# A cross-attention kernel on one core: a second PSUM bank for the second head's context, softmax weights read back in one transfer, and both value products ahead of the contexts

## The chip, the core and the metric

The kernel runs on one core of one Trainium2 chip. The number that counts is the device time in microseconds (us) of one execution. A core has TensorE (PE, matrix products into PSUM), VectorE (DVE), ScalarE (ACT), GpSimd (POOL) and SyncE (SP), whose queue issues the DMA transfers here. Each engine works through its own list of instructions in order, and the lists are tied by semaphores that the program waits for. PSUM has eight banks of 512 fp32 values per partition, named here by number.

## The reference, cut to what matters

Sixteen sequences of 128 tokens and 512 features pass one RWKV layer (its time mix and channel mix come first in the kernel and are not touched) and then a block with two cross-attentions and an MLP. The context `xf` is 128 tokens per sequence:

```
def _cross_attention(q_in, kv_in, wq, bq, wk, bk, wv, bv, wo, bo, bias_k, bias_v):
    qh = (q_in @ wq + bq).reshape(b, q_len, H, K)          # H = 16 heads of K = 128
    kh = (kv_in @ wk + bk).reshape(b, t, H, K)
    vh = (kv_in @ wv + bv).reshape(b, t, H, K)
    kh = concatenate([kh, bias_k], axis=1)                 # a 129th key and value
    vh = concatenate([vh, bias_v], axis=1)
    weights = softmax(einsum('bqhk,bthk->bhqt', qh, kh) / sqrt(K))
    ctx = einsum('bhqt,bthk->bqhk', weights, vh)
    return ctx @ wo + bo
...
x = x + attention_1(layer_norm(x), xf); x = x + attention_2(layer_norm(x), xf)
x = x + gelu(layer_norm(x) @ w_fc1 + b_fc1) @ w_fc2 + b_fc2
```

## The kernel before, in words

`cross_attend` works in units. A unit is two heads of four sequences (a "quad", 512 tokens). Sixteen sequences make two halves `h`; a half has two quads; each attention `st` has 8 pairs of heads `g`. That makes 2 x 2 x 8 x 2 = 64 attention units. Products that must be exact are made of three passes with split operands (`_hi` and `_lo`, helper `mm3`, lines 60 to 62).

Each engine has its own function for one step of the pipeline, and the step joins two units: `A`, whose attention is finished, and `C`, whose queries, keys and values are made meanwhile. `slot(A, C)` is the step inside a half's attention: 7 turns of a loop, 2 steps each, four times, 56 in all. The other 8 are at borders, where a layer norm for the next stage goes between: `second` (4 times, the second quad of a stage), `turn` (2, from attention 1 to 2) and `mlp_turn` (2, to the MLP; the last of them has no unit `C`). On PE `second` and `turn` are both `passing`.

The order within a step is written out by hand on each engine. On PE in `slot`: the scores of A's two heads among queries and keys of C, then `value(C, 0)` (bank 2), `context(A, 0)`, half of `value(C, 1)` (bank 3), `context(A, 1)`, the other half, and `attended(A)`, the output product. One `value` call is 24 matmuls of 256 columns.

Softmax weights take a detour. ScalarE writes `exp` into `pr` with queries on partitions; VectorE normalises (line 1741) and transposes blocks of 32 x 32 (line 1745) into `pb`; SyncE's queue stores `pb` to DRAM (line 1441) and loads it back with whole keys on partitions into `pT` (line 1446, a tile that the profile calls `xres`). `context` (line 1991, `ca_ps<-xres,xq`) multiplies it with the values `vT` (`xq`) into `BANK_PV`, bank 7, for both heads. ScalarE reads that bank into `ct_hi` (line 1559), VectorE reads it again for `ct_lo` (line 1749), and `context` waits, by `ct_split`, until the head before it has been read. `attended` waits for `ct_lo` of head 0 before its first matmul and of head 1 before its fourth (line 60, `ca_ps<-ca_wo_hi,ca_ct_hi`).

Of the kernel before, what the change touches and what calls it, by code (L numbers as in the profile page):

```python
# [20 lines left out]
ACT = mybir.ActivationFunctionType  # L21
# [4 lines left out]
P = 128  # L26
# [1261 lines left out]
def cross_attend(nc, io, x3, out, common, early):  # L1288
    HT = 8
    G = NH // 2  # L1290
    KW = L + 1
    BANK_Q, BANK_K, BANK_O, BANK_SC, BANK_PV = 0, 1, 2, 5, 7
    TB = 32
    LN_BANKS = (0, 1, 5, 6)
    FC_BANKS = ((4, 7), (5, 6))
# [1 line left out]
    with ExitStack() as ctx:  # L1297
# [119 lines left out]
        def head_col(U, kind, hd):  # L1417
            return hv[:, bass.ds(U.g * 2 + ((U.st * 5 + HV[kind]) * NH + hd), 1)]
# [4 lines left out]
        def _(sp):  # L1423
# [13 lines left out]
            def probs_across(A, hd):  # L1437

                sp.wait_ge(blocks_ready, A.n * 2 + (hd + 1))
                sp.wait_ge(pt_in[hd], A.n * 64)  # L1440
                sp.dma_start(pb_dram[hd], pb[hd][:].rearrange("p j b s -> p (j b s)")).then_inc(blocks_out[hd], 16)
                if A.n > 0:
                    sp.wait_ge(pv_full, A.n * 2 + (hd - 1))
                sp.wait_ge(blocks_out[hd], A.n * 16 + 16)
                for j in range(4):
                    sp.dma_start(pT[hd][TB * j:TB * j + TB, :].rearrange("r (i x) -> r i x", i=4),  # L1446
                                 pb_dram[hd].rearrange("(i r) (j x) -> j r i x", i=4, j=4)[j]).then_inc(pt_in[hd], 16)

            def probs(h, i, quad):
                for hd in range(2):  # L1450
# [77 lines left out]
        def _(act):  # L1528
# [27 lines left out]
            def context_hi(A, hd):  # L1556
                act.wait_ge(pv_full, A.n * 2 + (hd + 1))
                wait_apart(act)
                act.activation(cT[hd][0][:], ps[:, BANK_PV, :], ACT.Identity, bias=head_col(A, "bias_v", hd)).then_inc(ct_hi, 1)  # L1559

            def roots(ln):
                act.wait_ge(stats_ready, ln + 1)
                act.activation(std[:, :], mv[:, :, 1], ACT.Sqrt, bias=eps[:]).then_inc(std_ready, 1)
# [35 lines left out]
            def second(A, C):  # L1599
                exps(A, 0)  # L1600
                key_out(C, 0)
                split_one(wo, so, wo_in, wo_hi, C.wq)
                exps(A, 1)
                key_out(C, 1)
                roots(C.ln)
                context_hi(A, 0)
                split_one(wk, sk, wk_in, wk_hi, C.wkv + 1)
                context_hi(A, 1)
                norm_hi(C.ln, C.st, 1)
                query_out(C, 0, BANK_Q)  # L1610
# [96 lines left out]
        def _(v):  # L1707
# [29 lines left out]
            def normalise(A, hd):  # L1737
                v.wait_ge(exp_done, A.n * 2 + (hd + 1))
                v.reciprocal(rss[hd][:], sms[hd][:]).then_inc(rs_done, 1)
                v.wait_ge(rs_done, A.n * 2 + (hd + 1))  # L1740
                v.tensor_tensor(pr[hd][:, :, 0:L], pr[hd][:, :, 0:L],  # L1741
                                rss[hd][:].rearrange("p (a b) -> p a b", b=1).broadcast_to([P, 4, L]), ALU.mult).then_inc(norm_done, 1)
                v.wait_ge(norm_done, A.n * 2 + (hd + 1))
                v.wait_ge(blocks_out[hd], A.n * 16)
                v.transpose(pb[hd][:].rearrange("p j b s -> p b j s"), pr[hd][:, :, 0:L].rearrange("p b (j s) -> p b j s", s=TB)).then_inc(blocks_ready, 1)  # L1745

            def context_lo(A, hd):
                v.wait_ge(ct_hi, A.n * 2 + (hd + 1))
                v.scalar_tensor_tensor(out=cT[hd][1][:], in0=ps[:, BANK_PV, :], scalar=head_col(A, "bias_v", hd),  # L1749
                                       in1=cT[hd][0][:], op0=ALU.add, op1=ALU.subtract).then_inc(ct_split, 1)  # L1750

            def add_output(U, b):
# [55 lines left out]
            def second(A, C):  # L1808
                row_max(A, 0)
                if C.h == 1 and C.st == 0:  # L1810
                    v.wait_ge(x_in[1], 32)
                if C.st == 1:
                    v.wait_ge(o_out, A.o * 4)
                norm_stats(C.ln, C.h, 1)
                normalise(A, 0)
                row_max(A, 1)
                split_one(wo, so, wo_hi, wo_split, C.wq)
                normalise(A, 1)
                norm_apply(C.ln, C.h, 1)
                value_out(C, 0)  # L1820
                context_lo(A, 0)
                split_one(wk, sk, wk_hi, wk_split, C.wkv + 1)
                value_out(C, 1)
                context_lo(A, 1)
                norm_lo(C.ln, C.st, 1, A)
                split_q(C.wq + 1, 0)
                split_q(C.wq + 1, 1)
# [26 lines left out]
            def turn(A, C):  # L1854
                row_max(A, 0)
                v.wait_ge(o_out, A.o * 4)
                norm_stats(C.ln, C.h, 0)
                normalise(A, 0)
                row_max(A, 1)
                split_one(wv, sv, wv_hi, wv_split, C.wkv)  # L1860
                normalise(A, 1)
                key_col(C, 0)
                key_col(C, 1)
                norm_apply(C.ln, C.h, 0)
                value_out(C, 0)
                context_lo(A, 0)
                value_out(C, 1)
                context_lo(A, 1)
                norm_lo(C.ln, C.st, 0, A)

# [4 lines left out]
            def mlp_turn(A, C, M):  # L1875
# [66 lines left out]
        def _(pe):  # L1942
# [41 lines left out]
                ins.then_inc(sc_full, 1)  # L1984

            def context(A, hd):
                pe.wait_ge(pt_in[hd], A.n * 64 + 64)
                pe.wait_ge(v_out, A.n * 2 + 2)
                pe.wait_ge(ct_split, A.n * 2 + hd)
                for b in range(4):  # L1990
                    ins = pe.matmul(ps[:, BANK_PV, b * L:(b + 1) * L], vT[A.quad][:, b, hd * P:(hd + 1) * P],  # L1991
                                    pT[hd].rearrange("p (i b s) -> p b i s", i=4, b=4)[:, b], start=True, stop=True)
                ins.then_inc(pv_full, 1)

# [39 lines left out]
            def passing(A, C):  # L2034
# [51 lines left out]
            def mlp_turn(A, C, M):  # L2086
# [10 lines left out]
                if C is not None:  # L2097
# [132 lines left out]
```

## Time and profile before

| | before |
|---|---|
| median of 3 runs | 3030.14 us (3027.85 to 3033.89) |
| profiled execution, own time | 3028.64 us |
| span of its instructions | 3026.8 us |
| PE busy | 2836.7 us, 94% |
| DVE busy | 1860.2 us, 61% |
| ACT busy | 1092.0 us, 36% |
| POOL busy | 535.2 us, 18% |
| mean granted clock of PE | 0.978 |

The time mix and channel mix fill the first 900 us, cross-attention and MLP the rest. Busy time is a sum over stages; whether an engine holds up another is read from what its idle time ended on. In a timeline row the bracket gives the idle time of the engine before the instruction and what ended it; matmuls are pipelined, so the start of one to the start of the next is their pace.

### The profile page before, as it was taken

How to read it: one execution, taken by the hardware profiler on the slowest of the kernel's cores; microseconds unless marked ns; L12 is line 12 of the kernel's file. 1: busy time of each engine (PE TensorE's matmuls, PEld its weight loads, DVE VectorE, ACT ScalarE, POOL GpSimd, SP SyncE). 2: the span in 40 equal slices, each digit the busy share in tenths (PEclk: the TensorE clock that was granted, in tenths of full speed). 3: DMA queues.
4: the chain of work that ended last, by engine and by line, in shares of the span. 5: the costliest groups of instructions: out<-in, count | busy, mean ns of one | idle time of the engine just before them, and what ended most of it. 6: DMA issues, size and time to landing. Idle time of an engine off the chain costs nothing.

```text
span 3026.8 us, 40813 instructions
## 1 busy us (share of the span) xinstructions
PE 2836.7 (94%) x14352; PEld 2122.0 (70%) x14352; DVE 1860.2 (61%) x2743; ACT 1092.0 (36%) x2409; POOL 535.2 (18%) x373
## 2 busy tenths in 40 slices
PE   5989898997989999999999999999999999999799
PEld 2333333334778888888888878788888888888687
DVE  5989989897765444465444574564444654444644
ACT  3232323223434334343333343343343443433332
POOL 2857667572010000000000010010000000000100
PEclk8999899998999999999999999999999999999899
DMA  5010010111242222222222211132222222222111
GB/s 161 1 29 28 18 39 2 55 42 42 83 164 91 76 97 80 79 83 75 97 80 74 92 60 63 56 103 75 97 80 88 79 70 97 80 88 71 46 52 56
DMA packets 146370, 215.69 MB, mean 71 GB/s; under 512 B 16176, under 2 KB 82736, under 8 KB 145168
## 3 DMA queue, kind: packets, MB, share of 16 engines
q1 hardware_dynamic: 143408, 210.73, 20.9%
q0 software_dynamic: 2880, 3.94, 0.6%
q8 instruction: 43, 0.70, 0.1%
q14 instruction: 39, 0.32, 0.0%
HBM read 164.53 MB, written 46.14 MB: 70 GB/s over the span
## 4 chain that ended last, share of the span: by engine, by line
PE 61%; DVE 4%; ACT 2%; issue 1%; DMA 1%; SPq 0%; ACTq 0%; DVEq 0%
PE ca_ps L60 18%; PE ca_ps L62 17%; PE ca_ps L61 17%; PE ca_ps L1991 4%; PE ca_ps L1982 4%; DVE ca_ct_lo L1749 1%; ACT ca_ct_hi L1559 1%; DVE ca_stats L68 1%; DMA xres<-pb_dram 1%; DMA pb_dram<-ca_pb 1%; PE ca_ps L2018 1%; SPq L1446 0%; DVE ca_pb L1745 0%; DVE ca_pr L1741 0%; ACT ca_pr L1552 0%
## 5 line engine op out<-in xcount | busy, mean ns | idle before, releaser
L1552 ACT ACTIVATE ca_pr<-ca_ps,ca_nb 128x129 f32<-128x129 f32 x512 | 181.0, 369 | 426.4 <-DVE ca_nb L1735 426.4
L60 PE MATMUL ca_ps<-ca_h_hi,ca_wq_hi 128*128 128x512 f32 x768 | 308.3, 401 | 4.2 <-DVE ca_h_lo L1780 3.7
L1505 POOL TENSOR_TENSOR ca_dv<-ca_bvr 128x256 f32<-128x256 f32 x32 | 23.6, 738 | 1601.5 <-DVE xq L1720 1442.0
L617 DVE TENSOR_TENSOR_SCAN tm_xn<-tm_wd,tm_vb 128x512 f32<-128x512 f32 x256 | 298.5, 1208 | 12.7
L62 PE MATMUL ca_ps<-ca_h_hi,ca_wq_lo 128*128 128x512 f32 x768 | 302.4, 394 | 0.0
L61 PE MATMUL ca_ps<-ca_h_lo,ca_wq_hi 128*128 128x512 f32 x768 | 301.3, 392 | 0.0
L60 PE MATMUL ca_ps<-ca_wv_hi,ca_ctx_hi 128*128 128x256 f32 x1024 | 296.3, 289 | 1.3 <-DVE ca_wv_lo L1715 1.3
L61 PE MATMUL ca_ps<-ca_wv_lo,ca_ctx_hi 128*128 128x256 f32 x1024 | 286.0, 279 | 0.0
L62 PE MATMUL ca_ps<-ca_wv_hi,ca_ctx_lo 128*128 128x256 f32 x1024 | 286.0, 279 | 0.0
L1749 DVE SCALAR_TENSOR_TENSOR ca_ct_lo<-ca_ps,ca_hv,ca_ct_hi 128x512 fp32r<-128x512 f32 x128 | 96.1, 751 | 278.1 <-ACT ca_ct_hi L1559 277.8
L60 PE MATMUL ca_ps<-ca_wo_hi,ca_ct_hi 128*128 128x512 f32 x640 | 255.3, 399 | 0.2 <-DVE raw L1755 0.2
L62 PE MATMUL ca_ps<-ca_wo_hi,ca_ct_lo 128*128 128x512 f32 x640 | 252.4, 394 | 0.0
L61 PE MATMUL ca_ps<-ca_wo_lo,ca_ct_hi 128*128 128x512 f32 x640 | 252.3, 394 | 0.0
L60 PE MATMUL ca_ps<-ca_ctx_hi,ca_wk_hi 128*128 128x512 f32 x512 | 208.7, 408 | 11.9 <-DVE ca_wk_lo L1715 7.9
L1755 DVE TENSOR_TENSOR ca_xres<-ca_xres,ca_ps 128x512 f32<-128x512 f32 x192 | 131.9, 687 | 117.3 <-PE ca_ps L62 115.3
L62 PE MATMUL ca_ps<-ca_ctx_hi,ca_wk_lo 128*128 128x512 f32 x512 | 202.6, 396 | 0.0
L61 PE MATMUL ca_ps<-ca_ctx_lo,ca_wk_hi 128*128 128x512 f32 x512 | 202.2, 395 | 0.0
L1755 DVE TENSOR_TENSOR raw<-raw,ca_ps 128x512 f32<-128x512 f32 x192 | 132.0, 687 | 112.1 <-PE ca_ps L62 110.2
L1559 ACT ACTIVATE ca_ct_hi<-ca_ps,ca_hv 128x512 fp32r<-128x512 f32 x128 | 88.1, 688 | 307.0 <-PE ca_ps L1991 307.0
L60 PEld LDWEIGHTS ca_ps<-ca_wv_hi,ca_ctx_hi 128*128 128x128 f32 x1024 | 193.0, 188 | 4.7 <-issue 2.1
L61 PEld LDWEIGHTS ca_ps<-ca_wv_lo,ca_ctx_hi 128*128 128x128 f32 x1024 | 192.8, 188 | 2.6
L62 PEld LDWEIGHTS ca_ps<-ca_wv_hi,ca_ctx_lo 128*128 128x128 f32 x1024 | 194.4, 190 | 0.0
(232 smaller groups left out, 5926.1 us busy)
## 6 DMA issues: line engine op xcount, KB each, us to landing
pb_dram<-ca_pb SPq DMA_DIRECT2D x128, 256.0 KB, 2.0
xres<-pb_dram SPq DMA_DIRECT2D x512, 64.0 KB, 1.9
ca_sq<-in_wq SPq DMA_DIRECT2D x49, 512.0 KB, 5.4
ca_so<-in_wo SPq DMA_DIRECT2D x48, 512.0 KB, 3.7
ca_sk<-in_wk SPq DMA_DIRECT2D x33, 512.0 KB, 6.5
ca_sv<-in_wv SPq DMA_DIRECT2D x32, 512.0 KB, 4.0
x_dram<-xres SPq DMA_DIRECT2D x8, 1024.0 KB, 4.2
ca_bvr<-in_bvb SPq DMA_DIRECT2D x32, 256.0 KB, 4.2
```

Source lines behind the costliest of these rows:

```text
L60: pe.matmul(out, lhs[0], rhs[0], start=first, stop=False)
L61: pe.matmul(out, lhs[0], rhs[1], start=False, stop=False)
L62: return pe.matmul(out, lhs[1], rhs[0], start=False, stop=last)
L68: v.bn_stats(stats[:, b, :], x4[:, b, :]).then_inc(bn_done, 1)
L617: v.tensor_tensor_scan(state[t % 2][:, d, :], wd[:, g].rearrange("p b t -> p (b t)"), pair[:, d, :], 0.0, ALU.mult, ALU.add).then_inc(scan ...
L1552: ins = act.activation(pr[hd][:, b, :], ps[:, BANK_SC + b // 2, o:o + KW], ACT.Exp, bias=nbs[hd][:, b:b + 1], scale=SCALE, accum_out=sms[h ...
L1559: act.activation(cT[hd][0][:], ps[:, BANK_PV, :], ACT.Identity, bias=head_col(A, "bias_v", hd)).then_inc(ct_hi, 1)
L1749: v.scalar_tensor_tensor(out=cT[hd][1][:], in0=ps[:, BANK_PV, :], scalar=head_col(A, "bias_v", hd), in1=cT[hd][0][:], op0=ALU.add, op1=ALU ...
L1755: v.tensor_tensor(xres[U.h][:, U.quad * 4 + b, :], xres[U.h][:, U.quad * 4 + b, :], ps[:, BANK_O + b % 2, :], ALU.add).then_inc(o_out, 1)
L1982: ins = pe.matmul(ps[:, BANK_SC + b // 2, o:o + KW], qT[hd][:, b * L:(b + 1) * L], kT[hd][:, b, :], start=True, stop=True)
L1991: ins = pe.matmul(ps[:, BANK_PV, b * L:(b + 1) * L], vT[A.quad][:, b, hd * P:(hd + 1) * P], pT[hd].rearrange("p (i b s) -> p b i s", i=4, ...
L2018: ins = pe.transpose(ps[:, LN_BANKS[c], b * P:(b + 1) * P], lt[:, b, c * P:(c + 1) * P], ident[:])
```

## The change

Four edits, all in `cross_attend`:

- Head 1's context goes to bank 4 (`CTX_BANKS = (7, 4)`). `context` no longer waits for the head before it, but for the same head of the unit before (`ct_split` at `A.n * 2 + (hd - 1)` in place of `A.n * 2 + hd`).
- The transpose on VectorE reads the keys with a stride of four elements (every fourth key to a block) instead of 32 in a row. Row `r` of block `j` is then key `4r + j`, and the load back is one transfer over 128 partitions instead of four over 32 each.
- At the borders (`passing`, `mlp_turn`) PE makes both `value` products before both `context` products; VectorE and ScalarE follow (in ScalarE's `second` the split of `wk` comes before both `context_hi`).
- In the last `mlp_turn`, which has no unit C, PE makes the layer norm's transposes before the two contexts.

```diff
-    BANK_Q, BANK_K, BANK_O, BANK_SC, BANK_PV = 0, 1, 2, 5, 7
+    BANK_Q, BANK_K, BANK_O, BANK_SC = 0, 1, 2, 5
+    CTX_BANKS = (7, 4)
...
-                sp.wait_ge(pt_in[hd], A.n * 64)
+                sp.wait_ge(pt_in[hd], A.n * 16)
...
-                for j in range(4):
-                    sp.dma_start(pT[hd][TB * j:TB * j + TB, :].rearrange("r (i x) -> r i x", i=4),
-                                 pb_dram[hd].rearrange("(i r) (j x) -> j r i x", i=4, j=4)[j]).then_inc(pt_in[hd], 16)
+                sp.dma_start(pT[hd].rearrange("p (i x) -> p i x", i=4),
+                             pb_dram[hd].rearrange("(i r) (j x) -> (r j) i x", i=4, j=4)).then_inc(pt_in[hd], 16)
...
-                act.activation(cT[hd][0][:], ps[:, BANK_PV, :], ACT.Identity, bias=head_col(A, "bias_v", hd)).then_inc(ct_hi, 1)
+                act.activation(cT[hd][0][:], ps[:, CTX_BANKS[hd], :], ACT.Identity, bias=head_col(A, "bias_v", hd)).then_inc(ct_hi, 1)
...  (ScalarE, second)
+                split_one(wk, sk, wk_in, wk_hi, C.wkv + 1)
                 context_hi(A, 0)
-                split_one(wk, sk, wk_in, wk_hi, C.wkv + 1)
                 context_hi(A, 1)
...  (VectorE, normalise)
-                v.transpose(pb[hd][:].rearrange("p j b s -> p b j s"), pr[hd][:, :, 0:L].rearrange("p b (j s) -> p b j s", s=TB)).then_inc(blocks_ready, 1)
+                v.transpose(pb[hd][:].rearrange("p j b s -> p b j s"), pr[hd][:, :, 0:L].rearrange("p b (s j) -> p b j s", s=TB)).then_inc(blocks_ready, 1)
...  (VectorE, second; turn and mlp_turn likewise)
                 value_out(C, 0)
-                context_lo(A, 0)
                 split_one(wk, sk, wk_hi, wk_split, C.wkv + 1)
                 value_out(C, 1)
+                context_lo(A, 0)
                 context_lo(A, 1)
...  (TensorE, context)
-                pe.wait_ge(pt_in[hd], A.n * 64 + 64)
+                pe.wait_ge(pt_in[hd], A.n * 16 + 16)
                 pe.wait_ge(v_out, A.n * 2 + 2)
-                pe.wait_ge(ct_split, A.n * 2 + hd)
+                if not (isinstance(A.g, int) and A.n == 0):
+                    pe.wait_ge(ct_split, A.n * 2 + (hd - 1))
...  (TensorE, passing)
                 value(C, 0, A.o * 4 - 1 if C.n > 1 else 0)
+                value(C, 1, A.o * 4 if C.n > 1 else 0)
                 context(A, 0)
-                value(C, 1, A.o * 4 if C.n > 1 else 0)
                 context(A, 1)
...  (TensorE, mlp_turn)
-                context(A, 0)
-                if C is not None:
                     value(C, 1, A.o * 4)
-                context(A, 1)
-                pe.wait_ge(exp_done, A.n * 2 + 2)
-                norm_transpose(M.ln, A.n * 2 + 2, A.n * 2 + (2 if C is None else 4))
+                    context(A, 0)
+                    context(A, 1)
+                    pe.wait_ge(exp_done, A.n * 2 + 2)
+                    norm_transpose(M.ln, A.n * 2 + 2, A.n * 2 + 4)
+                else:
+                    pe.wait_ge(exp_done, A.n * 2 + 2)
+                    norm_transpose(M.ln, A.n * 2 + 2, A.n * 2 + 2)
+                    context(A, 0)
+                    context(A, 1)
```

Inside `slot` no instruction changes its place on any engine; only what `context` waits for does. The three places where rows move follow, with the semaphores that each row waits for.

SyncE's queue in the first border step (`ca_pb0` and `ca_pb1` are the two heads' blocks, `xres` is `pT`), before:

```order
L1441 DMA pb_dram<-ca_pb0 128x512 [waits ca_pt_in0,ca_blocks_ready]
L1446 DMA xres<-pb_dram 32x4x128 [waits ca_blocks_out0]
L1446 DMA xres<-pb_dram 32x4x128 x3
L1441 DMA pb_dram<-ca_pb1 128x512 [waits ca_pt_in1,ca_blocks_ready]
L1446 DMA xres<-pb_dram 32x4x128 [waits ca_blocks_out1]
```

and of the change:

```order
L1442 DMA pb_dram<-ca_pb0 128x512 [waits ca_pt_in0,ca_blocks_ready]
L1446 DMA xres<-pb_dram 128x4x128 [waits ca_blocks_out0]
L1442 DMA pb_dram<-ca_pb1 128x512 [waits ca_pt_in1,ca_blocks_ready]
L1446 DMA xres<-pb_dram 128x4x128 [waits ca_blocks_out1]
L1480 DMA ca_so<-in_wo 128x1024 [waits ca_wo_split]
```

Each head has one load where it had four.

VectorE in `second` (line 1720 takes a value product out of PSUM, line 1749 is `ct_lo`, line 1775 begins the layer norm's second half), before:

```order
L1720 TENSOR_TENSOR xq<-ca_ps,ca_dv 128x512 [waits ca_dv_ready,ca_v_full]
L1749 SCALAR_TENSOR_TENSOR ca_ct0_lo<-ca_ps,ca_hv,ca_ct0_hi 128x512 [waits ca_ct_hi]
L1715 TENSOR_TENSOR ca_wk_lo<-ca_sk,ca_wk_hi 128x1024 [waits ca_wk_hi]
L1720 TENSOR_TENSOR xq<-ca_ps,ca_dv 128x512 [waits ca_dv_ready,ca_v_full]
L1749 SCALAR_TENSOR_TENSOR ca_ct1_lo<-ca_ps,ca_hv,ca_ct1_hi 128x512 [waits ca_ct_hi]
```

and of the change:

```order
L1720 TENSOR_TENSOR xq<-ca_ps,ca_dv 128x512 [waits ca_dv_ready,ca_v_full]
L1715 TENSOR_TENSOR ca_wk_lo<-ca_sk,ca_wk_hi 128x1024 [waits ca_wk_hi]
L1720 TENSOR_TENSOR xq<-ca_ps,ca_dv 128x512 [waits ca_dv_ready,ca_v_full]
L1749 SCALAR_TENSOR_TENSOR ca_ct0_lo<-ca_ps,ca_hv,ca_ct0_hi 128x512 [waits ca_ct_hi]
L1749 SCALAR_TENSOR_TENSOR ca_ct1_lo<-ca_ps,ca_hv,ca_ct1_hi 128x512 [waits ca_ct_hi]
```

Both `ct_lo` now stand behind the second value.

TensorE in the last `mlp_turn` (line 1991 is the context, line 2018 the layer norm's transposes), before:

```order
L1991 MATMUL ca_ps<-xres,xq 128x128 [waits ca_ct_split,ca_v_out,ca_pt_in0]
L1991 MATMUL ca_ps<-xres,xq 128x128 x3
L1991 MATMUL ca_ps<-xres,xq 128x128 [waits ca_ct_split,ca_v_out,ca_pt_in1]
L1991 MATMUL ca_ps<-xres,xq 128x128 x3
L2018 MATMUL ca_ps<-ident,raw 128x128 [waits ca_k_out,ca_xn0_ready,ca_q_out,ca_exp_done]
```

and of the change, from the last transposes on:

```order
L2018 MATMUL ca_ps<-ident,raw 128x128 [waits ca_xn0_ready]
L2018 MATMUL ca_ps<-ident,raw 128x128 x3
L1991 MATMUL ca_ps<-xres,xq 128x128 [waits ca_ct_split,ca_v_out,ca_pt_in0]
L1991 MATMUL ca_ps<-xres,xq 128x128 x3
L1991 MATMUL ca_ps<-xres,xq 128x128 [waits ca_ct_split,ca_v_out,ca_pt_in1]
```

All sixteen transposes now come ahead of both contexts.

## Rows read from the trace of the kernel before

**Rows 1.** The page: busy time of TensorE, and the chain by engine.

```profile
PE 2836.7 (94%) x14352; PEld 2122.0 (70%) x14352; DVE 1860.2 (61%) x2743; ACT 1092.0 (36%) x2409; POOL 535.2 (18%) x373
...
PE 61%; DVE 4%; ACT 2%; issue 1%; DMA 1%; SPq 0%; ACTq 0%; DVEq 0%
```

**Rows 2.** Waits of TensorE: us in total, times, longest.

```profile
PE ca_ps L1991 <- DVE ca_ct_lo L1749: 29.0, 55, 0.5
PE ca_ps L1991 <- DMA xres<-pb_dram: 17.7, 12, 6.0
```

**Rows 3.** Timeline of TensorE in one `slot`: start us, us, what [idle before].

```profile
1310.24 1.05 PE L1991 MATMUL ca_ps<-xres,xq 128*128 128x128 f32 x8
1311.05 0.36 PE L60 MATMUL ca_ps<-ca_wv_hi,ca_ctx_hi 128*128 128x256 f32 x1
...
1312.43 0.28 PE L62 MATMUL ca_ps<-ca_wv_hi,ca_ctx_lo 128*128 128x256 f32 x1
1313.25 1.13 PE L1991 MATMUL ca_ps<-xres,xq 128*128 128x128 f32 x8 [0.54 <-DVE ca_ct_lo L1749]
1314.13 0.37 PE L60 MATMUL ca_ps<-ca_wv_hi,ca_ctx_hi 128*128 128x256 f32 x1
...
1316.28 0.46 PE L60 MATMUL ca_ps<-ca_wo_hi,ca_ct_hi 128*128 128x512 f32 x1
```

**Rows 4.** Timeline of VectorE in the same `slot`.

```profile
1312.35 0.75 DVE L1749 SCALAR_TENSOR_TENSOR ca_ct_lo<-ca_ps,ca_hv,ca_ct_hi 128x512 fp32r<-128x512 f32 x1 [2.70 <-ACT ca_ct_hi L1559]
...
1313.62 1.22 DVE L1715 TENSOR_TENSOR ca_wk_lo<-ca_sk,ca_wk_hi 128x1024 fp32r<-128x1024 f32 x1
...
1315.43 0.75 DVE L1749 SCALAR_TENSOR_TENSOR ca_ct_lo<-ca_ps,ca_hv,ca_ct_hi 128x512 fp32r<-128x512 f32 x1 [0.60 <-ACT ca_ct_hi L1559]
```

**Rows 5.** Timeline of SyncE's queue in the same `slot`, head 1.

```profile
1306.02 0.34 SPq L1441 DMA_DIRECT2D pb_dram<-ca_pb  x1
1308.08 1.89 SPq L1446 DMA_DIRECT2D xres<-pb_dram  x4
```

**Rows 6.** DMA issues: count, KB each, median us to landing.

```profile
xres<-pb_dram SPq DMA_DIRECT2D x512, 64.0 KB, 1.9
ca_sq<-in_wq SPq DMA_DIRECT2D x49, 512.0 KB, 5.4
...
ca_bvr<-in_bvb SPq DMA_DIRECT2D x32, 256.0 KB, 4.2
```

**Rows 7.** Window around one head's four loads; at the end clock, DMA share, GB/s.

```profile
1302.00:1305.50 3.50, 3.50 (x17) 2.88 (x16) 1.84 (x4) 2.62 (x10) 0.00 (x0) 1.00 0.27 75
```

**Rows 8.** Groups of VectorE by line and shape: busy us, mean ns.

```profile
L1745 DVE STREAM_TRANSPOSE ca_pb<-ca_pr 128x512 f32<-128x512 f32 x128 | 91.1, 712 | 9.7
L1715 DVE TENSOR_TENSOR ca_wo_lo<-ca_so,ca_wo_hi 128x1024 fp32r<-128x1024 f32 x48 | 58.6, 1222 | 7.6 <-ACT ca_wo_hi L1535 7.6
L1786 DVE TENSOR_TENSOR ca_ctx_lo<-ca_xres,ca_ctx_hi 128x2048 fp32r<-128x2048 f32 x4 | 10.2, 2560 | 2.9 <-ACT ca_ctx_hi L1581 2.9
```

**Rows 9.** Timeline of the first border step, all engines.

```profile
924.43 0.71 DVE L1745 STREAM_TRANSPOSE ca_pb<-ca_pr 128x512 f32<-128x512 f32 x1
...
925.06 0.66 DVE L1733 TENSOR_REDUCE ca_mx<-ca_ps 128x4 f32<-128x516 f32 x1
...
931.24 1.73 SPq L1446 DMA_DIRECT2D xres<-pb_dram  x4
...
934.58 1.16 PE L1991 MATMUL ca_ps<-xres,xq 128*128 128x128 f32 x8
```

**Rows 10.** Timeline of SyncE's queue in the last `mlp_turn`, head 1.

```profile
2824.11 1.73 SPq L1446 DMA_DIRECT2D xres<-pb_dram  x4
```

**Rows 11.** Timeline of TensorE and VectorE in the last `mlp_turn`.

```profile
2827.38 2.07 PE L1991 MATMUL ca_ps<-xres,xq 128*128 128x128 f32 x8 [3.31 <-DMA xres<-pb_dram]
...
2830.30 0.75 DVE L1749 SCALAR_TENSOR_TENSOR ca_ct_lo<-ca_ps,ca_hv,ca_ct_hi 128x512 fp32r<-128x512 f32 x1 [4.63 <-ACT ca_ct_hi L1559]
...
2832.61 0.39 PE L60 MATMUL ca_ps<-ca_wo_hi,ca_ct_hi 128*128 128x512 f32 x1
```

More of the change, by code:

```diff
@@ L1744, in normalise @@
                 v.wait_ge(blocks_out[hd], A.n * 16)
-                v.transpose(pb[hd][:].rearrange("p j b s -> p b j s"), pr[hd][:, :, 0:L].rearrange("p b (j s) -> p b j s", s=TB)).then_inc(blocks_ready, 1)
+                v.transpose(pb[hd][:].rearrange("p j b s -> p b j s"), pr[hd][:, :, 0:L].rearrange("p b (s j) -> p b j s", s=TB)).then_inc(blocks_ready, 1)
             def context_lo(A, hd):
                 v.wait_ge(ct_hi, A.n * 2 + (hd + 1))
-                v.scalar_tensor_tensor(out=cT[hd][1][:], in0=ps[:, BANK_PV, :], scalar=head_col(A, "bias_v", hd),
+                v.scalar_tensor_tensor(out=cT[hd][1][:], in0=ps[:, CTX_BANKS[hd], :], scalar=head_col(A, "bias_v", hd),
                                        in1=cT[hd][0][:], op0=ALU.add, op1=ALU.subtract).then_inc(ct_split, 1)
@@ L1865, in turn @@
                 value_out(C, 0)
+                value_out(C, 1)
                 context_lo(A, 0)
-                value_out(C, 1)
                 context_lo(A, 1)
@@ L1891, in mlp_turn @@
                     value_out(C, 0)
+                    value_out(C, 1)
                 context_lo(A, 0)
-                if C is not None:
-                    value_out(C, 1)
                 context_lo(A, 1)
@@ L1986, in context @@
             def context(A, hd):
-                pe.wait_ge(pt_in[hd], A.n * 64 + 64)
+                pe.wait_ge(pt_in[hd], A.n * 16 + 16)
                 pe.wait_ge(v_out, A.n * 2 + 2)
-                pe.wait_ge(ct_split, A.n * 2 + hd)
+                if not (isinstance(A.g, int) and A.n == 0):
+                    pe.wait_ge(ct_split, A.n * 2 + (hd - 1))
                 for b in range(4):
-                    ins = pe.matmul(ps[:, BANK_PV, b * L:(b + 1) * L], vT[A.quad][:, b, hd * P:(hd + 1) * P],
+                    ins = pe.matmul(ps[:, CTX_BANKS[hd], b * L:(b + 1) * L], vT[A.quad][:, b, hd * P:(hd + 1) * P],
                                     pT[hd].rearrange("p (i b s) -> p b i s", i=4, b=4)[:, b], start=True, stop=True)
@@ L2095, in mlp_turn @@
                     value(C, 0, A.o * 4 - 1)
-                context(A, 0)
-                if C is not None:
                     value(C, 1, A.o * 4)
-                context(A, 1)
-                pe.wait_ge(exp_done, A.n * 2 + 2)
-                norm_transpose(M.ln, A.n * 2 + 2, A.n * 2 + (2 if C is None else 4))
+                    context(A, 0)
[7 more added lines that the diff above has]
+                    context(A, 1)
                 attended(A, A.n * 2 + (2 if C is None else 4))
```

## The prediction, made before the changed kernel was run

> **What bounds the kernel now.** I read the page first: TensorE is busy 94% of the span and makes 61% of the chain that ended last, all other engines together some 6% [rows 1]. So only idle time of TensorE is worth much. The second view is the list of TensorE's waits [rows 2], in which the context line 1991 stands twice: 55 short waits for VectorE's `ct_lo`, 29.0 us together, and 12 waits for the load of the softmax weights, 17.7 us with one of 6.0 us. The third view is the timeline of one `slot`, to see what such a wait costs in starts of matmuls and what would be late next [rows 3 to 5]; the fourth is the timeline of a border step [rows 9] and of the last one [rows 10, 11]. There are 56 slots and 8 border steps. I treat them apart, because in a slot the weights have long landed when `context` comes, and in a border step `context` waits for them.
>
> **Part 1: head 1's own bank, in the 56 slots.** The value matmuls of 256 columns start 0.12 us apart. The last before the second context starts at 1312.43, so the context would start at 1312.55 without a wait. It starts at 1313.25 [rows 3], just behind the end of head 0's `ct_lo` at 1312.35 + 0.75 = 1313.10 [rows 4]: 0.70 us lost. The group is also slower when it starts from a standstill, since the next matmul follows 1314.13 - 1313.25 = 0.88 us later, where for head 0, which waits for nothing, it follows 1311.05 - 1310.24 = 0.81 us later [rows 3]. That is 0.77 us a slot. The changed wait is for head 1 of the unit before, read a whole step earlier, so the whole 0.77 us goes: 56 x 0.77 = 43.1 us.
>
> What is late next? Three things follow the context. First the weights themselves: head 1's four loads issue from 1308.08 to about 1309.55, and the last lands 1.9 us later, about 1311.45 [rows 5, 6], 1.1 us ahead of 1312.55. So the DMA does not take the wait over. Second `ct_lo` of head 1, which the fourth output matmul waits for. That matmul starts at 1316.28, and `ct_lo` ends at 1315.43 + 0.75 = 1316.18 [rows 3, 4]: it is already the limit, without slack. It starts 2.18 us after the context; with the context at 1312.55, and its group 0.07 us quicker, it is wanted at 1314.66. In every second slot VectorE is then still in the split of `wk`, 1313.62 + 1.22 = 1314.84 [rows 4]. A following instruction starts about 0.08 us before the end of the one ahead (924.43 + 0.71 against 925.06, rows 9), so `ct_lo` is 0.10 us late in 28 slots: 2.8 us given back. Third the output products, which keep their distance to `ct_lo`. One of the 56 waits is missing from the 55 because in that slot a late load ended it; there I count 0.6 us less. Part 1 brings 43.1 - 2.8 - 0.6 = 39.7 us.
>
> The wait amounts for head 0 need one register instruction more on TensorE's sequencer in the slot. It runs while 24 value matmuls are still queued, and I cost it at nothing; were it exposed it would be under 0.1 us a slot.
>
> **Part 2: one load instead of four.** The bytes and pieces stay: 256 KB a head, 512 pieces of 512 bytes. Four issues take 1.89 or 1.73 us [rows 5, 9], so the last leaves three quarters of that, 1.3 us or more, after the first and lands 1.9 us after that, 3.2 us in all [rows 6]. One transfer has all pieces at once. In a window that holds nothing but these loads the 16 engines are busy for 0.27 of 3.50 us, 0.96 us each [rows 7]. A quarter of that, 0.24 us, is inside the 1.9 us that one small load takes, so one large load takes 1.9 + 0.72 = 2.6 us: 0.6 us earlier. Bounds: 1.9 us if the pieces overlap fully; above, the loads of 256 and 512 KB that take 4.2 and 5.4 us [rows 6]. Those stand in the queue behind other large loads, so I take 2.6. In the slots this buys only slack. SyncE's queue is free 1.3 us earlier, which nobody waits for.
>
> **Part 3: the transpose with stride four.** It takes 0.71 us now [rows 8]. No row shows a long read of single elements 16 bytes apart. Below, 0.71 us; above, 2.56 us, VectorE's row with four times the elements. I take the row with twice as many, 1.22 us [rows 8], as if every element cost one more cycle, since no two neighbours in the read stand side by side any more: 0.51 us more each, 1.02 us for two heads in a row. In the slots the load's slack of 1.1 + 0.6 us covers it and VectorE, busy 61% [rows 1], is idle 2.70 us ahead of `ct_lo` [rows 4]; it costs nothing there. In a border step VectorE's `row_max` of head 1 starts in the same breath as head 0's transpose ends (925.06, rows 9), so head 1's load comes 1.02 us later.
>
> The Trainium skill, "SBUF — State Buffer", in its note on cachelines, says that consecutive reads inside one line of 16 bytes run at full bandwidth and that each read that crosses to a new line pays a penalty, which this stride does at every element. It gives no price and no run here shows it yet; by that rule the transpose is slower and by the present row it stays at 0.71 us, with the two results below.
>
> **Part 4: both values, then the contexts.** In a border step the second context starts at 934.58 as head 1's load lands (931.24 + 1.3 + 1.9, rows 9, 6). That landing sets the step's end whichever way the values stand, so the new order moves idle time from before context 0 to before context 1 and brings nothing by itself. The landing moves by +1.02 (part 3) and -0.63 (part 2): 0.39 us later, in 7 border steps 2.7 us lost. The two `ct_lo` behind the second value have the 16 transposes of the norm as cover.
>
> **Part 5: the last `mlp_turn`.** Its load issues from 2824.11 [rows 10]; by the above it would issue at 2825.13 and land at 2827.73. Before, `ct_lo` of head 1 ended 2831.05 - 2827.38 = 3.67 us after the context's start, and then the transposes and the first output matmuls put the fourth output matmul at 2832.61 [rows 11]. Now the transposes are done before, and that matmul only needs `ct_lo`: 2827.77 + 3.67 + 0.1 = 2831.55. That is 1.1 us gained.
>
> **Sum.** 39.7 - 2.7 + 1.1 = 38.1 us. The profiled execution took 3028.64 us, so 2990.5; the median of the runs is 1.5 us above it, so 2992 us.
>
> **Rivals.**
>
> *The strided transpose costs nothing.* Then the 7 border steps gain 0.63 us each (4.4 us) and the last 2832.61 - (2824.11 + 2.6 + 3.8) = 2.1 us: 39.7 + 4.4 + 2.1 = 46.2 us, 2984 us. For it: the only row of this instruction, with the same number of elements. Against it only that no row shows such a read.
>
> *It costs as much as four times the elements*, 2.56 us: two of them put head 1's load 3.7 us later, 3.1 us a border step after part 2, 7 x 3.1 + 2 = 24 us lost. In the slots the landing at 1308.08 + 1.85 + 2.6 = 1312.53 is just in time. Gain 16 us, 3014 us.
>
> *The one large load is slow, and TensorE waits for it in every slot.* This is the case on the other side. All 512 pieces come at once, with four to a partition from places 64 KB apart, as `ca_sq` has 512 pieces and takes 5.4 us. In a slot the load has 1312.55 - 1308.08 - 0.51 = 3.96 us. A load of 4.2 us, as `ca_bvr`'s, stalls each slot 0.24 us, takes the 0.07 us of the standstill back and costs a border step 1.02 + 4.2 - 3.2 = 2.0 us: 56 x 0.46 - 2.8 - 8 x 2.0 = 7 us gained; from about 4.3 us on nothing is. At 5.4 us a slot stalls 1.44 us and loses 0.74 us against now, 41 us in 56, and the border steps lose 8 x 3.2 = 26 us: 3097 us. Against it: the same pieces are served now in 0.96 us of engine time.
>
> *The wait only moves to `ct_lo` of head 1.* Then the fourth output matmul waits 0.7 us in each slot and the time stays near 3030. Against it: VectorE and ScalarE follow the context at a fixed distance and are idle before it (0.60 us, rows 4), so they come earlier with it.
>
> **How the numbers follow.** A measurement of this kernel tells about 0.2%, 6 us, from no change. Forecast (2986 to 3001): 0.50. Free transpose (2978 to 2986): 0.32. Dear transpose or a load of 3 to 4 us (3001 to 3024): 0.10. Slow load of 4.2 to 4.4 us, or the wait that only moves (3024 to 3036): 0.04. Slow load above: 0.04. So faster 0.92, same 0.04, slower 0.04. The range is 2977 to 3006: it holds the first two cases and the start of the third.
>
> **What would show it.** Right: TensorE's waits have no row of line 1991 for `ct_lo`; in a slot the second context starts 0.12 us after the value matmul before it; TensorE's idle time falls by about 40 us. The row of the one load says 2.6 us to landing; the transpose's row says 1.22 us or 0.71 us and decides between the first two cases; a border step waits some 2 us for the load, before the second context. Wrong: line 1991 waits for `xres<-pb_dram` in the slots, or line 60 for `ca_ct_lo` by more than 0.2 us each.

## The result, and the profile after

| | before | after |
|---|---|---|
| median of the first comparison | 3029.34 us (3027.85 to 3033.89, 4 runs) | 2989.41 us (2984.19 to 2992.39, 4 runs) |
| median of the second comparison | 3028.38 us (3025.96 to 3031.15, 7 runs) | 2986.10 us (2979.10 to 2990.05, 4 runs) |
| profiled execution, own time | 3028.64 us | 2984.19 us |
| span | 3026.8 us | 2982.4 us |

The ratio of after to before is 0.9864, interval 0.9846 to 0.9882, in the first comparison and 0.9863, 0.9846 to 0.9879, in the second: 40 to 42 us faster. 2992 us was forecast. The profiled execution is the fastest of its four, so its span fell by 44.4 us, more than the median. One of the 17 executions of the kernel before that stand beside the first four experiments took 7142.07 us and is not in their ratios.

The page of after, against [rows 1]:

```profile
PE 2822.3 (95%) x14352; PEld 2116.9 (71%) x14352; DVE 1902.8 (64%) x2743; ACT 1092.2 (37%) x2409; POOL 535.0 (18%) x373
...
PE 64%; DVE 3%; DMA 1%; ACT 1%; issue 1%; DVEq 0%; ACTq 0%; SPq 0%
```

TensorE's idle time went from 3026.8 - 2836.7 = 190.1 us to 160.1 us, and its busy time fell by 14.4 us with the same count of matmuls. So the idle time fell by 30 us and not by the 40 that the prediction named as a sign. [rows 3] show why. The last value matmul ahead of the second context is drawn 0.28 us long, while the pace is 0.12 us, so 0.16 us of the 0.70 us lost stand in the profile as busy and 0.54 us as idle. The slower start of a waiting group (drawn 1.13 against 1.05 us) is busy time too. Over the 56 slots 29.6 us of idle and 11.1 us of busy time went.

TensorE's waits in after (total us, times, longest), against [rows 2]:

```profile
PE ca_ps L2018 <- DVE raw L1768: 9.9, 4, 7.0
PE ca_ps L1991 <- DMA xres<-pb_dram: 8.0, 6, 2.5
...
PE ca_ps L60 <- DVE ca_ct_lo L1749: 0.7, 2, 0.5
```

The row of line 1991 for `ct_lo`, 29.0 us in 55 waits, is gone, and no other of that size has come. What is left for the load are the border steps. The 7.0 us in the first row is the last `mlp_turn`. There TensorE waited 6.0 us for head 0's load before ([rows 2]); now the transposes come first, and they wait about as long for VectorE's layer norm (line 1768).

The same `slot` on TensorE, against [rows 3]:

```profile
1300.59 1.05 PE L1991 MATMUL ca_ps<-xres,xq 128*128 128x128 f32 x8
...
1302.78 0.28 PE L62 MATMUL ca_ps<-ca_wv_hi,ca_ctx_lo 128*128 128x256 f32 x1
1302.90 1.05 PE L1991 MATMUL ca_ps<-xres,xq 128*128 128x128 f32 x8
1303.71 0.36 PE L60 MATMUL ca_ps<-ca_wv_hi,ca_ctx_hi 128*128 128x256 f32 x1
...
1305.90 0.49 PE L60 MATMUL ca_ps<-ca_wo_hi,ca_ct_hi 128*128 128x512 f32 x1
```

The second context starts 0.12 us behind the value matmul ahead of it, where it was 0.82, and the next matmul follows after 0.81 us, where it was 0.88. VectorE in the same `slot`, against [rows 4]:

```profile
1302.70 0.75 DVE L1749 SCALAR_TENSOR_TENSOR ca_ct_lo<-ca_ps,ca_hv,ca_ct_hi 128x512 fp32r<-128x512 f32 x1 [2.62 <-ACT ca_ct_hi L1559]
...
1303.97 1.22 DVE L1715 TENSOR_TENSOR ca_wk_lo<-ca_sk,ca_wk_hi 128x1024 fp32r<-128x1024 f32 x1
1305.10 0.75 DVE L1749 SCALAR_TENSOR_TENSOR ca_ct_lo<-ca_ps,ca_hv,ca_ct_hi 128x512 fp32r<-128x512 f32 x1
```

Head 1's `ct_lo` has no bracket any more: it comes straight behind the split of `wk` and ends at 1305.85, just before the fourth output matmul, which starts at 1305.90.

The queue and the load, against [rows 5, 6], and the transpose, against [rows 8]:

```profile
1296.84 0.32 SPq L1442 DMA_DIRECT2D pb_dram<-ca_pb  x1
1298.87 0.37 SPq L1446 DMA_DIRECT2D xres<-pb_dram  x1
```

```profile
xres<-pb_dram SPq DMA_DIRECT2D x128, 256.0 KB, 2.7
```

```profile
L1745 DVE STREAM_TRANSPOSE ca_pb<-ca_pr 128x512 f32<-128x512 f32 x128 | 141.9, 1109 | 9.7
```

Head 1's load lands about 1298.87 + 2.7 = 1301.6, 1.3 us before its context. The transpose takes 1.11 us, where it took 0.71.

**Where the time went.** I cut the traces at the first score matmul of each step (an `mlp_turn` ends at the first matmul of the MLP) and compare the lengths, in us against the kernel before:

| kernel | 56 slots | 4 `second` | 2 `turn` | first `mlp_turn` | last | in front of the units |
|---|---|---|---|---|---|---|
| after | -40.7 | +0.3 | -0.9 | -0.6 | -3.1 | +0.6 |
| after, again | -40.6 | +0.3 | -0.5 | -1.6 | -2.7 | -4.5 |
| bank alone | -39.5 | +0.7 | 0.0 | -0.1 | +0.4 | +5.2 |
| load alone | +1.3 | -0.2 | -0.8 | -1.4 | +0.2 | -0.4 |
| four loads | -40.4 | +2.4 | -0.3 | -1.6 | -2.6 | +0.9 |
| old order | -40.4 | +0.2 | -0.7 | -1.5 | +0.3 | +2.5 |
| old order in the last step | -39.6 | +1.9 | -0.4 | -1.5 | +0.5 | -0.3 |
| split of `wk` late | -37.2 | +0.4 | -0.3 | -0.5 | -2.3 | +0.1 |
| transposes between contexts | -40.1 | -1.9 | +0.1 | +0.2 | -3.0 | +1.0 |
| half of them, in `second` | -40.8 | -1.9 | -0.7 | -0.5 | -2.7 | -0.3 |
| the same, VectorE reordered | -39.3 | -0.4 | -0.3 | -1.4 | -2.9 | -0.3 |
| eight loads | +29.3 | +24.1 | +11.6 | +4.8 | +1.0 | -0.9 |

The last column is time mix and channel mix, which no kernel here changes. It moves by up to 5 us from execution to execution, also for one and the same kernel. So effects of 1 to 4 us are read from the steps, not from the medians.

Two columns also carry a difference that comes from the granted clock and not from an edit alone. In the first `mlp_turn` TensorE waits 3.2 us for VectorE in every kernel. In before, after, bank_only, wk_late, ln_first and ln_half a stretch of 3.4 us at the lower clock (1.2 GHz) begins as that wait ends, and the step takes 27.4 to 28.2 us. In six other profiles the clock stays at 2.4 GHz there, and it takes 26.3 to 26.5 us; eight_loads, with its longer waits, stands apart. After and after_again are the same kernel, one of each kind:

```profile
1736.50 0.80 PE L60 MATMUL ca_ps<-ca_ctx_hi,ca_wk_hi 128*128 128x512 f32 x1 [3.19 <-DVE ca_ctx_lo L1786]
```

```profile
1731.77 0.51 PE L60 MATMUL ca_ps<-ca_ctx_hi,ca_wk_hi 128*128 128x512 f32 x1 [3.19 <-DVE ca_ctx_lo L1786]
```

So some 1 us of that column is the clock, and with the lower clock on both sides after gains 0.6 us there. The last `second` has the same split: eight_loads aside, it is at 1.2 GHz for 3.4 us in four_loads and old_last alone, which explains most of their +2.4 and +1.9 us.

### The profile page after: what moved, and what is told of

Read it like the earlier page. It is cut to its first block, busy times and chain, and to the rows that moved or that the text cites. A ratio compares the mean times of both kernels' runs of the same rounds, so it can differ in the third digit from the quotient of the medians.

```text
span 2982.4 us, 40485 instructions
## 1 busy us (share of the span) xinstructions
PE 2822.3 (95%) x14352; PEld 2116.9 (71%) x14352; DVE 1902.8 (64%) x2743; ACT 1092.2 (37%) x2409; POOL 535.0 (18%) x373
## 4 chain that ended last, share of the span: by engine, by line
PE 64%; DVE 3%; DMA 1%; ACT 1%; issue 1%; DVEq 0%; ACTq 0%; SPq 0%
PE ca_ps L60 19%; PE ca_ps L62 19%; PE ca_ps L61 19%; PE ca_ps L1991 4%; PE ca_ps L1981 4%; DMA xres<-pb_dram 1%; DVE ca_stats L68 1%; DVE ca_pb L1745 0%; DMA pb_dram<-ca_pb 0%; PE ca_ps L2018 0%; ACT ca_pr L1552 0%; DVE ca_mx L1733 0%; DVE ca_pr L1741 0%; DVE ca_ctx_lo L1786 0%; DVE raw L1755 0%
```

## The experiments

Each was compared with the kernel before on the same chip.

**bank_only.** The kernel before with head 1's bank alone.

```diff
-ps[:, BANK_PV, ...
+ps[:, CTX_BANKS[hd], ...
-pe.wait_ge(ct_split, A.n * 2 + hd)
+if not (isinstance(A.g, int) and A.n == 0):
+    pe.wait_ge(ct_split, A.n * 2 + (hd - 1))
```

> The kernel before with only the second bank and the loosened wait; four loads, the old transpose and the old order at the borders stay. Theory A (nearly all of the gain is the 56 slots' wait for ct_lo): 56 x 0.77 us less 0.1 us in 28 slots, so 40 us faster, about 2989 to 2991 us; in a slot the second context starts 0.12 us after the value matmul before it, and the border steps and the last mlp_turn are as before. Rival B (the four loads would land too late once the context may start earlier, so the one load carries part of the gain): TensorE waits for the load in the slots by 0.3 us or more, 15 to 20 us of gain missing, about 3008 us.

2990.33 us (2987.02 to 2995.24), ratio 0.9862, interval 0.9845 to 0.9878. The waits have no `ct_lo` row:

```profile
PE ca_ps L1993 <- DMA xres<-pb_dram: 18.7, 14, 6.9
```

Theory A holds: this edit alone gives the whole ratio, and its 56 slots account for it, with -39.5 us. No run has the second bank with the old wait, so the two halves of this edit are not told apart by a run; the rows of [rows 3] and of after account for the gain by the wait alone.

**load_only.** The kernel before with the other key order: one load and the strided transpose, the bank shared.

```diff
-for j in range(4):
-    sp.dma_start(pT[hd][TB * j:TB * j + TB, :]..., ...[j]).then_inc(pt_in[hd], 16)
+sp.dma_start(pT[hd]..., ...).then_inc(pt_in[hd], 16)
-"p b (j s) -> p b j s"
+"p b (s j) -> p b j s"
```

> The kernel before with only the strided transpose and the one load; one bank, old order. Theory A: nothing in the slots, since the wait for ct_lo stays; in the 8 border steps head 1's load comes 0.8 us later for two slower transposes (1.11 against 0.71 us each) and lands 0.6 us sooner, so 0.1 to 0.2 us lost in each: 3029 to 3032 us, no difference that can be measured. Rival B (the load gives a gain of its own): 5 to 10 us faster, 3020 to 3025 us.

3027.65 us (3024.45 to 3036.08, 12 runs), ratio 0.9989, interval 0.9979 to 1.0. The load gives no gain of its own that these runs can tell, as theory A said; the small loss that it forecast at the borders did not come either. The old wait is whole:

```profile
PE ca_ps L1990 <- DVE ca_ct_lo L1748: 29.5, 56, 0.5
PE ca_ps L1990 <- DMA xres<-pb_dram: 16.3, 13, 6.5
```

**four_loads.** The changed kernel with the key order and the four loads of before; bank and new order stay.

> The changed kernel with four loads and the old transpose put back: second bank and new order alone. Theory A: the slots keep their whole gain (40 us); in the border steps the landing is 0.1 to 0.2 us sooner than in the changed kernel; 2988 to 2990 us, as the changed kernel. Rival B (the one load carries part of the gain): 3000 us or more. The transpose's row should read 0.71 us.

2991.41 us (2986.79 to 2995.65), ratio 0.9873, interval 0.9858 to 0.9889. Its transpose is back at 711 ns. Of the +2.4 us in `second`, 2.3 are in the last of the four. There the store takes 3.67 us until the load can be issued (2.92 in after), so context 1 starts 0.5 us later in the step than in after; behind it the granted clock is at 1.2 GHz for 3.4 us, and the 16 transposes take 3.19 us in place of 1.91. The single load is worth nothing that can be told, as theory A said.

**old_border.** Bank and single load, every step in the order of before.

> The changed kernel with the order before at all 8 border steps and in the last mlp_turn: second bank and one load alone. Theory A: the order of values and contexts brings nothing, because head 1's landing sets the end of a border step; only the last mlp_turn loses its 1 to 3 us: 2990 to 2993 us. Rival C (the new order is worth 0.5 us or more at each border): 2995 us or more.

2987.25 us (2984.75 to 2988.99), ratio 0.9852, interval 0.9838 to 0.9867: below the 2990 to 2993 of theory A. By the steps the order is worth nothing in the seven borders, as part 4 said, and 3 us in the last step, which the medians do not show.

**after_again.** The changed kernel a second time.

> The changed kernel once more, beside which the three others of this call are read. Both theories: 2989 us, within 4 us (one profiled execution of it took 2984.2, its median was 2989.4). Step sums against the kernel before: the 56 slots -40 us, the seven borders together -1 to -3, the last turn to the MLP -3. Theory A (the part of the program in front of the slots varies from execution to execution by several us): the front differs by over 2 us from the earlier profile of the same kernel while the slots stay at -40 to -41. Theory B (the single execution profiled was typical): the front is within 1 us.

2986.10 us; the columns of the table agree with the first profile within 1 us (the largest difference is the first `mlp_turn`, with the clock), while the front moved by 5.0 us. Theory A holds.

**old_last.** After with the old order in the last `mlp_turn` alone.

```diff
+    context(A, 0)
+    context(A, 1)
     norm_transpose(M.ln, A.n * 2 + 2, A.n * 2 + 2)
-    context(A, 0)
-    context(A, 1)
```

> The changed kernel with the last turn to the MLP in the order of before: both contexts ahead of the layer norm's transposes. Theory A (the new order there is worth what the profiles showed): the last step gets about 3 us longer, 2.0 of it because the stretch at half the granted clock is 17 us long instead of 10, so 2 to 4 us slower than the changed kernel. Theory B (the half clock there depends on the execution and not on the order: it fell to 10 us in one kernel with the old borders elsewhere and to 17 in others): the stretch is 10 us here too and the last step is longer by 1 us or less.

2989.28 us (2988.11 to 2991.99), ratio 0.9871, interval 0.9854 to 0.9887: 3.2 us above after in the same comparison. The last step is 3.2 to 3.6 us longer. Windows of that step (us, busy of five engines, granted clock, DMA share, GB/s), first of this kernel, then of after:

```profile
2776.00:2793.00 17.00, 8.15 (x34) 7.73 (x35) 7.84 (x15) 5.02 (x13) 4.93 (x4) 0.50 0.27 93
2793.00:2797.00 4.00, 4.00 (x18) 3.21 (x17) 3.55 (x6) 2.97 (x6) 0.00 (x0) 0.99 0.00 0
```

```profile
2774.00:2784.00 10.00, 3.14 (x15) 3.17 (x16) 6.33 (x12) 3.09 (x10) 1.84 (x2) 0.50 0.26 86
2784.00:2788.00 4.00, 3.32 (x22) 2.48 (x20) 1.43 (x3) 2.09 (x4) 3.10 (x3) 1.00 0.49 180
```

With the old order both contexts and the transposes run at 1.2 GHz. In after only the transposes do, and those run while head 1's weights are still on their way to DRAM and back. Over all thirteen profiles the time at 1.2 GHz in that step is 17.1 us in each of the five with the old order there, and 10.2 to 13.7 us in each of the eight with the new. Theory A holds.

**wk_late.** After, with VectorE's split of `wk` behind head 1's `ct_lo`.

```diff
 context_lo(A, 0); value_out(C, 0)
-if C.quad == 1: split_one(wk, ...)
 context_lo(A, 1); value_out(C, 1)
+if C.quad == 1: split_one(wk, ...)
```

> The changed kernel with VectorE's split of the next key weights behind context_lo of head 1 and value_out of the second half, in the slots of the second batch quad. Theory A (that split stands in front of head 1's lower half in every second slot and makes the fourth output matmul 0.10 us late there): 28 slots gain 0.10 us each, 2 to 3 us faster than the changed kernel. Theory B (the 0.10 us is a start-up interval that the split has no part in, or the split's lateness holds up the key weights' next load and their first matmul): no gain, or up to 0.3 us lost in each of the 28 following steps (8 us).

2988.64 us (2984.46 to 2991.26), ratio 0.9865, interval 0.9848 to 0.9881. Neither theory is right as it stands. In the 28 slots the output matmuls behind the fourth start 0.09 us earlier, as A said, but the third output then starts 0.05 us later than in after and the fourth output 0.15 us later, and these slots are 3.9 us longer in all. VectorE shows why:

```profile
1305.21 0.75 DVE L1749 SCALAR_TENSOR_TENSOR ca_ct_lo<-ca_ps,ca_hv,ca_ct_hi 128x512 fp32r<-128x512 f32 x1 [0.95 <-ACT ca_ct_hi L1559]
1305.88 0.68 DVE L1720 TENSOR_TENSOR xq<-ca_ps,ca_dv 128x512 f32<-128x512 f32 x1
1306.48 1.22 DVE L1715 TENSOR_TENSOR ca_wk_lo<-ca_sk,ca_wk_hi 128x1024 fp32r<-128x1024 f32 x1
1307.61 1.50 DVE L1755 TENSOR_TENSOR raw<-raw,ca_ps 128x512 f32<-128x512 f32 x2
```

The split now stands in front of the addition that empties the first output bank (line 1755), which the third output waits for. The 0.10 us of part 1 is real, and this is not the way to get it. So there was a loss, as theory B allowed, but through another wait than the ones it named.

**ln_first.** After, with the layer norm's 16 transposes between the two contexts in the borders, to fill the wait for head 1's load.

```diff
 context(A, 0)
+pe.wait_ge(exp_done, ...); norm_transpose(...)
 context(A, 1)
-pe.wait_ge(exp_done, ...); norm_transpose(...)
```

> The changed kernel with the layer norm's transposes between the two contexts in the seven borders, where TensorE waits about 1.6 us for head 1's load. Theory A (that wait is the load's alone and can be filled): the wait in front of context 1 goes, 16 transposes (1.66 us) fill it, but the outputs behind context 1 then wait for its halves, about 0.9 us in front of their fourth matmul: 0.7 us gained in each border, 5 us in all, 2984 us. Theory B (the outputs wait as long as was gained, or the transposes come late from VectorE's normalisation): within 1 us of the changed kernel.

2987.83 us (2981.63 to 2991.03), ratio 0.9864, interval 0.9846 to 0.9882. In place of the load's wait came the one that theory A priced, under 1 us but in every border:

```profile
PE ca_ps L60 <- DVE ca_ct_lo L1749: 6.7, 12, 1.0
PE ca_ps L1991 <- DMA xres<-pb_dram: 1.0, 2, 0.7
```

The four `second` gained 2.2 us against after; the turns and the first `mlp_turn`, whose wait for the load was only 0.1 to 0.5 us in after, lost 1.8 us together. Theory B in the sum.

**ln_half.** Half of the transposes between the contexts, half behind, in the four `second` only.

> The changed kernel with half of the layer norm's transposes (8 of 16, 0.83 us) between the two contexts, and half behind, in the four border steps that lead from the first to the second batch quad, the three turns left as they are. With all 16 between the contexts these four gained 0.5 us each and the turns, whose wait is only 0.4 to 0.8 us, lost 0.4 to 0.9. Theory A (the wait for the load, 1.6 us, and the wait for head 1's halves, about 0.9, can share the transposes): 0.8 us gained in each of the four, 3 us. Theory B (one of the two waits comes back whole): 0.5 us or less each.

2981.61 us (2980.89 to 2985.70, 5 runs), ratio 0.9843, interval 0.9830 to 0.9857. It is the fastest kernel here, but its interval overlaps that of after, and the steps show 2.2 us in `second`, 0.5 us each: less than theory A's 0.8, no more than `ln_first`, so nearer theory B. The rest of the median's distance is no effect that the steps show.

**best2.** As ln_half, and VectorE in `second` takes head 1's row maximum and both normalisations first, the split of `wo` last.

```diff
 norm_stats(C.ln, C.h, 1)
-normalise(A, 0); row_max(A, 1); split_one(wo, ...); normalise(A, 1)
+row_max(A, 1); normalise(A, 0); normalise(A, 1); split_one(wo, ...)
```

> As the kernel with half the transposes between the contexts, and on VectorE in the same four steps the row maximum of head 1 ahead of the normalisation of head 0, and both normalisations ahead of the split of the output weights. Theory A (head 1's chain through the exponentials then starts 0.9 us earlier and its store leaves 1.0 us earlier): the wait for head 1's load goes, the outputs start 1.5 us earlier in each of four steps, 6 us below the changed kernel, about 2983 us, though one profile will show it more surely than the median. Theory B (head 0, which is then stored 1.5 us later, takes over the wait, since its context has only about 0.4 us to spare): context 0 waits up to 1 us and the gain is 2 us or less.

2984.23 us (2981.37 to 2990.94), ratio 0.9853, interval 0.9836 to 0.9871. Its four `second` gained 0.7 us against after: theory B's size, but not its cause, as context 0 did not wait. SyncE's queue in one of them:

```profile
1348.48 0.33 SPq L1442 DMA_DIRECT2D pb_dram<-ca_pb  x1
1350.52 0.38 SPq L1446 DMA_DIRECT2D xres<-pb_dram  x1
1350.99 0.46 SPq L1442 DMA_DIRECT2D pb_dram<-ca_pb  x1
1353.95 0.37 SPq L1446 DMA_DIRECT2D xres<-pb_dram  x1
```

Head 1's store leaves 0.47 us behind head 0's load and takes 2.96 us until its own load can be issued. In the four `second` of this kernel that time is 3.00, 2.96, 3.02 and 3.90 us; in after, where the store leaves 2.4 us behind the load, it is 1.98, 2.02, 2.02 and 2.92 us. So the store loses about 1 us of what it gained in time of issue. That the other head's load is in its way is the likely reason; no run separates it from the rest of the new order.

**eight_loads.** After, with the one load cut into eight of 16 partitions, so that it lands later.

> The changed kernel with the probabilities' way back in eight loads of 16 partitions in place of one, same bytes and same transpose: a later landing, made on purpose, to measure how much room the single load has. Theory A (SP issues one load in 0.43 us, so the last of eight is issued 3.4 us after the first and lands about 4.9 us from the first issue, where the one load lands at 2.7): 2.2 us later, head 1's load had 1.3 to 1.4 us of room in the slots, so each of the 56 slots loses 0.8 us and each of seven borders 2.2: 60 us, 3049 us, with head 1's context waiting for its load in every slot. Theory B (the room is larger than read, or the eight small loads land as early as the one): under 10 us lost and no wait for the load in the slots.

3099.38 us (3098.38 to 3103.20), ratio 1.0233, interval 1.0219 to 1.0247. A `slot` on the queue and on TensorE:

```profile
1293.72 3.58 SPq L1447 DMA_DIRECT2D xres<-pb_dram  x8
```

```profile
1298.77 1.16 PE L1992 MATMUL ca_ps<-xres,xq 128*128 128x128 f32 x8 [0.85 <-DMA xres<-pb_dram]
```

The last of eight lands 5.05 us after the first issue, as theory A said (4.9), and the slots lose 1.25 us each against after, 70 us. The seven borders lose 5.9 us each where 2.2 was expected. For one part the wait for the load in front of context 1 grew by 3.1 us on average and not by 2.2: head 1's store stands behind the eight issues of head 0's load and leaves at least 3.7 us after the first of them, where it was 2.4 us in most of them. A `turn` shows the other part:

```profile
1354.23 2.07 PE L1992 MATMUL ca_ps<-xres,xq 128*128 128x128 f32 x8 [4.55 <-DMA xres<-pb_dram]
1356.10 3.38 PE L2019 MATMUL ca_ps<-ident,raw 128*128 128x128 f32 x16
```

```profile
1346.00:1352.00 6.00, 3.25 (x27) 2.87 (x25) 3.08 (x6) 0.69 (x1) 4.89 (x4) 1.00 0.25 83
1352.00:1358.00 6.00, 3.77 (x17) 3.77 (x18) 0.75 (x1) 0.69 (x1) 0.06 (x1) 0.52 0.76 241
```

At the end of an idle stretch of 4.55 us the granted clock is at its lower level, 1.2 GHz, and context and transposes take 2.07 and 3.38 us in place of 1.16 and 1.91.

## Why the prediction was right, step by step

**Part 1, the bank: right.** 39.7 us were forecast for the 56 slots; after, after_again and bank_only show 40.7, 40.6 and 39.5. The gap of 0.70 us went and the 0.07 us of the standstill too. In the 28 slots with the split of `wk` head 1's `ct_lo` starts 2.20 us after its context, in the other 28 slots 2.09 us after it: late by the 0.10 us foreseen, for the reason foreseen. The one sign that failed is TensorE's idle time, for the prediction took all of the 0.70 us as idle, where [rows 3] already had 0.54.

**Part 2, the load: right.** 2.6 us were forecast, 2.7 measured. As said, nobody in the slots waits for it, and four_loads shows that it is worth nothing there.

**Part 3, the transpose: the mechanism right, the size too high.** 1.22 us was taken from the row with twice the elements, and 1.11 measured. The rule of the Trainium skill, "SBUF — State Buffer", in its note on cachelines, is that reads which cross to a new line of 16 bytes pay a penalty; the trace agrees with it, with +0.40 us for 512 elements. No run tries another stride, so that the lines are the cause is not shown. The rival of the free transpose falls by the same row.

**Part 4, the borders: the sum was too pessimistic.** 2.7 us were to be lost in seven; the profiles of after show 1.2 and 1.8 us gained. In the first border the issue of head 1's load comes 0.67 us later relative to head 0's transpose (932.45 - 924.97 = 7.48 against 931.24 - 924.43 = 6.81), not 1.02, and it lands 0.68 us faster (935.11 - 932.45 = 2.66 against 3.34). So the four `second` stand where they were. Three things make up the 0.35 us: the two transposes are 0.11 us shorter each than taken, instructions behind them overlap their end a little more, and the store returned 0.07 us sooner. The first `mlp_turn` gains 0.6 and 1.6 us, and the larger gain has the clock in it, which the prediction did not consider. The turns gain 0.9 and 0.5 us together, also with the load alone; why is open. The sign of about 2 us of waiting for the load came true in the four `second` (1.5 to 2.5 us), not in the other three borders (0.1 to 0.8 us): one reading of the first border was taken for all seven.

**Part 5, the last step: right in sign, too small.** 1.1 us forecast, 2.7 to 3.1 measured. Two terms were off, and their sum accounts for it. The first is the load. Counted from the step's first score matmul, context 1 was forecast at 2827.77 - 2810.32 = 17.45 us; it starts at 16.31 us in after and at 16.71 in after_again. The prediction had added the 1.02 us of part 3 to an issue at 13.79 us that was itself late: the store ahead of it took 3.44 us in the kernel before and 2.49 in after, where the load is issued at 13.57 us. The second is the clock. I took the 3.67 us from the context's start to the end of `ct_lo` from [rows 11], where the context runs at half the clock (2.07 us). In the new order the clock is back first, at 2784.01; context 1 starts at 2785.32 and `ct_lo` ends 2.75 us later, in after_again too:

```profile
2784.16 2.31 PE L1991 MATMUL ca_ps<-xres,xq 128*128 128x128 f32 x16
2786.96 0.47 PE L60 MATMUL ca_ps<-ca_wo_hi,ca_ct_hi 128*128 128x512 f32 x1 [0.49 <-DVE ca_ct_lo L1749]
...
2788.13 0.50 PE L60 MATMUL ca_ps<-ca_wo_hi,ca_ct_hi 128*128 128x512 f32 x1 [0.23 <-DVE ca_ct_lo L1749]
```

old_last confirms the second by taking the order back: it has 3.67 us again. So two steps failed: to carry over a duration measured at a clock that the change itself alters (0.9 us), and to build on the one late store of one execution (0.7 to 1.1 us).

**The rivals.** The wait that only moves to `ct_lo` did not come: line 60 waits 0.7 us in all. The slow load did not come either, but its price was about right: it put the break-even near 4.3 us, and at 5.05 us its working gives a stall of 5.05 - 3.96 = 1.09 us a slot and 0.07 us for the standstill, against 1.25 us measured. What it missed is the borders, where the clock falls and the queue holds head 1's store back.

**The whole.** The errors of parts 4 and 5 go the same way, 4 us and 2 us, and are less than the runs of one kernel differ by (2979 to 2992 us). It is the steps that confirm part 1. That the medians lie only 3 and 6 us below 2992, with parts 4 and 5 together 6 us off, is in part luck.

## What to carry to other kernels

When a tile in PSUM is read out between two uses by the bottleneck engine, price the wait in starts of matmuls in one step, add the slower restart, and multiply; then ask for each follower (the load, the read-out, the next product) how much later it already was than needed. Here that gave the gain within 1 us in 40, while the single load and the new order at the seven borders, each sensible on its own, moved work that nobody waited for.

A wait that cannot be avoided is best filled with work that would else come behind it, and only as far as it is long: the transposes that won 0.5 us against a wait of 1.6 us lost 0.4 to 0.8 us against waits of 0.1 to 0.5. And a duration taken from a stretch at the lower clock holds only while that stretch stays where it is.

## What the runs showed of the hardware that was not expected

- A `STREAM_TRANSPOSE` of 128x512 that reads single elements 16 bytes apart takes 1109 ns, against 711 in order: half the surcharge of twice the elements on VectorE would have been too little, the whole (1222 ns) too much.
- The clock follows small changes in the order of work: the same last step has 10.2 to 13.7 us at 1.2 GHz with the transposes in front of the contexts, 17.1 us with them behind, and in a `turn` a wait grown from under 1 us to 4.55 us brought the lower level where the clock had stayed at 2.4 GHz.
- The length of the wait alone does not say whether the clock falls. After the same wait of 3.19 us it fell in after and not in after_again, one and the same kernel; behind a wait of 2.53 us in the last `second` it fell in old_last, behind 2.54 us it did not in after. Such a fall costs about 1 to 1.6 us.
- A store of 256 KB issued 0.47 us behind a load of 256 KB on the same queue took 3.0 us until what waits for it could be issued, in three of four steps, against 2.0 where it was issued 2.4 us behind. The other cost of that queue is issue: eight small loads take 3.6 us of it.
